# Turning the rows of layer 1 by DMA, with the attention sums nine steps behind

## The chip, the cores and the metric

The kernel runs on one core of a Trainium2 chip. The metric is the device time of one execution in microseconds. A core has five engines with their own instruction queues that meet only by semaphores: TensorE (PE, matmuls), VectorE (DVE), ScalarE (ACT), GpSimd (POOL) and SyncE (SP, which here only issues DMAs). DMAs issued by one engine go into that engine's queue and are carried out by 16 shared DMA engines; q1 is SP's queue, q10 ACT's, q0 GpSimd's.

## The reference

Two graph layers over N = 3327 nodes with D = 256 features and a dense 0/1 matrix adj of N x N:

```python
h = relu(layernorm(x))
s_left, s_right = (h @ W_sa) @ a_left, (h @ W_sa) @ a_right
e = where(adj != 0, exp(-leaky_relu(s_left[:, None] + s_right[None, :], 0.01)), 0)
x_a = e / (e.sum(1) + 1e-5) @ (h @ W_sa)
x_b = adj @ (h @ W_gcnb) + b_gcnb
x = x + sigmoid(gate_a * x_a + gate_b * x_b)      # gates: sigmoids of projections of adj @ h and h
h = relu(layernorm(x))
x = x + relu(((dinv * (adj + I) * dinv) @ h + h) @ W1 + b1)
```

## The kernel before, in words

The nodes are 26 tiles of 128, taken as 13 pairs (PAIRS = 13, LAST = 12). float32 values are kept as two float16 (or bfloat16) numbers, a rounded first half (HI) and the rest (LO), and multiplied by several matmuls.

**Front of layer 1.** For each pair s: DVE takes the statistics of the rows (row_stats), POOL the inverse deviation, DVE the shift (minus_mean), ACT normalizes into hf (norm). PE turns hf by four float32 transposes into the PSUM tile tp (turn), ACT rounds tp into hTh (turned), DVE takes the rest into hTl (turned_second); both lie in hTx. PE then multiplies by the weights: dense(s), 12 matmuls of 512 columns into the two PSUM banks of dn, and project(s), 8 small ones into pw, the scores. ACT copies each bank of dn into HI (first_halves), DVE takes the rest into LO (second_halves); dense(s+1) waits for the same bank's second half. DVE takes the scores out of pw (take_scores).

**The sums of pair m.** For every neighbour pair u: ACT makes the scores' exponentials Z (leaky, expo), DVE masks them by the adjacency (mask) and splits them (split into E), PE sums: neighbours(m, u), 8 matmuls with adj into accA, and unit(m, u), 12 matmuls with Z and E into accE. The adjacency of pair m is loaded by POOL's DMAs (load_adj), turned by DVE (turn_adj, two chunks, six and seven pairs), and stored for layer 2 by SP (keep_adj). Output row sets m = 1 to 12 follow m = 0; neighbours(m+1, u) run between the units of m, except that all of neighbours(1, u) stand ahead of unit(1, 0).

**The order.** Every engine's program is written out by hand. The front is a loop over steps s; in it, PE does dense(s), turn(s+2), and from s = 4 on the sums of pair m = 0 four steps behind: neighbours(0, s-4), unit(0, s-5). keep_busy(n) are n filler matmuls on a constant tile whose results nobody reads.

**Layer 2** (names ending in 1) uses the other way of turning rows: ACT rounds hf into hfx (rounded1), DVE puts the rest beside it (rounded_second1), and SP turns both by one transposing DMA from hfx into hTx (turn_rows1), so that PE does no transposes there. The DMAs of SP ahead of all this are the loads of x, then bgrep and b1rep (two vectors of 256, each repeated on 128 partitions), which nobody needs before about 100 us.

## Time and profile before

| | us |
|---|---|
| runs of the kernel before (3) | median 614.05, 613.71 to 614.7 |
| the profiled execution | 614.12, span 612.3 |
| TensorE busy | 593.1 (97%) |
| VectorE busy | 429.1 (70%) |
| ScalarE busy | 358.2 (59%) |
| GpSimd busy | 258.0 (42%) |

Busy shares are of the whole span; the profile's windows give them stretch by stretch. All times in the rows below are microseconds from the span's start unless marked ns. A timeline row of PE shows the time until the result of a matmul is written; matmuls overlap, so the step from one start to the next is what one costs.

### The profile page before, as it was taken

The page shows a single profiled execution, that of the slowest core. Times are in us where ns is not written, and L with a number is a line of the kernel's source. Part 1 is how long each engine was busy: PE and PEld are TensorE (multiplying, and loading weights), DVE is VectorE, ACT ScalarE, POOL GpSimd, SP SyncE. Part 2 cuts the span into 40 slices and gives each one's busy share as a digit, 9 for nine tenths or more (in the row PEclk, how much of TensorE's full clock was granted, in tenths as well). Part 3 has the DMA queues.
Part 4 walks back from the last instruction along what each step waited for, and adds up shares of the span by engine and source line. Part 5 has one row for each costly group of instructions (what it writes and reads, how often), then busy time and mean ns, then how long its engine had stood idle before and what let it go on. Part 6 is the DMA issues. An engine that isn't in the chain of part 4 may idle for free.

```text
span 612.3 us, 13252 instructions
## 1 busy us (share of the span) xinstructions
PE 593.1 (97%) x5265; PEld 508.2 (83%) x5265; DVE 429.1 (70%) x826; ACT 358.2 (59%) x865; POOL 258.0 (42%) x360
## 2 busy tenths in 40 slices
PE   6778999999999999999999999999999999999996
PEld 4446678888888888888888888888888888888886
DVE  5897877999999999899989989988753222111111
ACT  3576767798978888787978788979642000000000
POOL 3637333453544434343534376313132284435433
PEclk9999999999999999999999999999999999999999
DMA  8907396976574656556564745010300386545401
GB/s 198 220 5 112 54 223 184 203 106 172 79 181 74 168 93 151 113 130 120 123 148 95 163 79 78 2 19 2 128 2 18 102 326 214 167 165 192 146 19 34
DMA packets 55801, 73.60 MB, mean 120 GB/s; under 512 B 20027, under 2 KB 47933, under 8 KB 54331
## 3 DMA queue, kind: packets, MB, share of 16 engines
q0 software_dynamic: 28544, 22.15, 25.5%
q1 hardware_dynamic: 24754, 46.42, 23.5%
q10 hardware_dynamic: 2441, 4.20, 2.2%
q8 instruction: 41, 0.67, 0.5%
q14 instruction: 21, 0.17, 0.1%
HBM read 69.31 MB, written 22.16 MB: 149 GB/s over the span
## 4 chain that ended last, share of the span: by engine, by line
PE 91%; DVE 4%; issue 2%; DMA 2%; ACT 1%; ACTq 0%; DVEq 0%
PE accA L759 12%; PE accE L781 12%; PE accE L783 12%; PE accE L782 12%; PE accA L760 12%; PE accA L825 7%; PE accA L826 7%; PE accE L826 4%; PE accE L825 4%; PE accA L733 1%; PE accA L735 1%; PE accA L734 1%; DMA late<-in_L_gnn_W_gcnb_dram 1%; PE pw L798 1%; PE accA L841 1%
## 5 line engine op out<-in xcount | busy, mean ns | idle before, releaser
L781 PE MATMUL accE<-HI,Z 128*128 128x257 f16 x676 | 184.3, 273 | 0.0
L783 PE MATMUL accE<-HI,E 128*128 128x257 f16 x676 | 184.1, 272 | 0.0
L782 PE MATMUL accE<-LO,Z 128*128 128x256 f16 x676 | 183.9, 272 | 0.0
L548 ACT ACTIVATE Z<-LO,sr 128x256 f32<-128x256 f32 x338 | 151.4, 497 | 33.4 <-PE accE L783 33.4
L759 PE MATMUL accA<-HI,adjT 128*128 128x260 f16 x676 | 154.0, 273 | 0.0
L760 PE MATMUL accA<-LO,adjT 128*128 128x258 f16 x676 | 154.0, 273 | 0.0
L557 ACT ACTIVATE Z<-Z,sr 128x256 f32<-128x256 f32 x338 | 150.0, 496 | 0.2
L1036 DVE TENSOR_TENSOR Z<-adjT,Z 128x512 f32<-128x512 bf16 x169 | 127.8, 756 | 15.3 <-ACT Z L557 14.3
L1042 DVE TENSOR_TENSOR E<-Z 128x512 bf16<-128x512 f32 x169 | 129.0, 763 | 5.8
L370 POOL DMA_DIRECT2D stage<-in_adj_dram x96 | 59.6, 657 | 89.5 <-DVE adjT L1028 85.1
L826 PE MATMUL accA<-LO,adjT 128*128 128x256 f16 x416 | 91.6, 272 | 0.0
L825 PE MATMUL accA<-HI,adjT 128*128 128x256 f16 x416 | 91.6, 273 | 0.0
L759 PEld LDWEIGHTS accA<-HI,adjT 128*128 128x128 bf16 x676 | 65.8, 97 | 9.2
L760 PEld LDWEIGHTS accA<-LO,adjT 128*128 128x128 bf16 x676 | 65.8, 97 | 8.8
L782 PEld LDWEIGHTS accE<-LO,Z 128*128 128x128 bf16 x676 | 65.9, 98 | 8.4
L781 PEld LDWEIGHTS accE<-HI,Z 128*128 128x128 bf16 x676 | 65.8, 97 | 8.4
L783 PEld LDWEIGHTS accE<-HI,E 128*128 128x128 bf16 x676 | 65.7, 97 | 8.5
L1028 DVE STREAM_TRANSPOSE adjT<-stage 128x768 uint32<-128x768 uint32 (+1 forms) x52 | 50.9, 1016 | 0.0
L449 POOL TENSOR_SCALAR wx<-wx 128x512 f32<-128x512 f32 x13 | 12.7, 980 | 82.0 <-ACT wx L579 81.9
L825 PE MATMUL accE<-HI,stage 128*128 128x256 f16 x208 | 45.7, 272 | 0.0
L826 PE MATMUL accE<-LO,stage 128*128 128x256 f16 x208 | 45.7, 273 | 0.0
L480 POOL TENSOR_TENSOR late<-HI,LO 128x512 f32<-128x512 f16 x13 | 20.0, 1535 | 58.6 <-DVE wx L1214 28.4
(129 smaller groups left out, 746.3 us busy)
## 6 DMA issues: line engine op xcount, KB each, us to landing
adjT_store<-adjT SPq DMA_DIRECT2D x11, 1664.0 KB, 6.1
stage<-in_adj_dram POOLq DMA_DIRECT2D x48, 192.0 KB, 5.0
stage<-in_adj_dram POOLq DMA_DIRECT2D x36, 224.0 KB, 5.4
adjT<-adjT_store SPq DMA_DIRECT2D x7, 896.0 KB, 4.8
adjT<-adjT_store SPq DMA_DIRECT2D x7, 768.0 KB, 5.8
stage<-adjT_store SPq DMA_DIRECT2D x4, 896.0 KB, 6.6
stage<-adjT_store SPq DMA_DIRECT2D x4, 768.0 KB, 5.4
out_dram<-late ACTq DMA_DIRECT2D x11, 256.0 KB
```

The source lines that it names most:

```text
L370: pool.dma_start(stage[32 * b:32 * b + 32, :, :, w0:w1_], src).then_inc(adj_in[c], 16)
L548: ins = act.activation(Z[:, n % RING, v], slw[:, m], ACT.Relu, bias=sr99[:, t:t + 1], scale=1.0 - SLOPE)
L557: ins = act.activation(Z[:, n % RING, v], Z[:, n % RING, v], ACT.Exp, bias=sr01[:, t:t + 1], scale=-1.0)
L759: pe.matmul(dst[:, 0:D + 4], w, HI[:, t, ONE:HIW], start=(t == 0), stop=False)
L760: ins = pe.matmul(dst[:, 2:D + 4], w, LO[:, t, D:LOW], start=False, stop=(t == TILES - 1))
L781: pe.matmul(dst[:, 0:D + 1], zhi, HI[:, t, 0:D + 1], start=(t == 0), stop=False)
L782: pe.matmul(dst[:, 0:D], zhi, LO[:, t, 0:D], start=False, stop=False)
L783: ins = pe.matmul(dst[:, 0:D + 1], zlo, HI[:, t, 0:D + 1], start=False, stop=(t == TILES - 1))
L825: pe.matmul(dst, w, HI1[:, t, :], start=(t == 0), stop=False)
L826: ins = pe.matmul(dst, w, LO1[:, t, :], start=False, stop=(t == TILES - 1))
L1036: dve.tensor_tensor(Z[:, n % RING], rows, Z[:, n % RING], ALU.mult).then_inc(mask_ok, 1)
L1042: dve.tensor_tensor(E2[:, n % RING], Z[:, n % RING], hi, ALU.subtract).then_inc(e2_ok, 1)
```

## The change

Pairs 0 to 2 are still turned by PE. From pair 3 on (BY_PE = 3) layer 1 does what layer 2 does: ACT's rounded and DVE's rounded_second split hf into hfx (now two buffers), SP's turn_rows turns it into hTx, and PE's dense and project wait for the DMA's semaphore (turned_in). The turn of pair i waits until dense(i-2), the last reader of the same half of hTx, is done. The sums of pair m = 0, with leaky, expo, mask and split, run nine steps behind the dense steps (BEHIND = 9) and not four. Statistics are taken one pair a step instead of in batches. The bias of the gates moves from DVE's take_scores into ACT's gate_exp. GpSimd's loads of the adjacency of pairs 1 and 2 and DVE's turn_adj move to later steps. The first store of the left scores is issued by ACT at s = 8. The comments that name an engine are added here.

```diff
-    BATCHES = [(0, 1), (1, 2), (2, 3), (3, 4), (4, 5), (5, 7), (7, 9), (9, PAIRS)]
+    BY_PE = 3
+    BEHIND = 9
...
+    def turn_count(i):
+        return 16 * len([j for j in range(BY_PE, i + 1) if j % 2 == i % 2])
...
-        hfx = sb("hfx", [P, 2, HALVES, 2, P], F16)
+        hfx = sb("hfx", [P, 2, 2, HALVES, 2, P], F16)
...
+            def turn_rows(i):                                        # sync
+                sp.wait_ge(hfl_ok, i - BY_PE + 1)
+                sp.wait_ge(dn_ps, 2 * i - 2)
+                sp.dma_start_transpose(hTx[:, i % 2].rearrange("p a h (e i) -> p (a h e) i", e=2),
+                                       hfx[:, i % 2].rearrange("p a h e d -> p (a h e d)")).then_inc(hT_in[i % 2], 16)
...
             sp.dma_start(bgrep[:], ...)
             sp.dma_start(b1rep[:], ...)
-
-            sp.wait_ge(adj_in[1], adj_count(1, 1))
+            for i in range(BY_PE, PAIRS):
+                turn_rows(i)
             spread_left(0)
             keep_adj(0)
+            store_left(1)
             spread_left(1)
...
-            loads = {4: (1, 0), 5: (1, 1), 9: (2, 0), 10: (2, 1)}    # gpsimd
+            inv_std(3)
+            inv_std(4)
+            loads = {BEHIND: (1, 0), BEHIND + 1: (1, 1)}
             for s in range(PAIRS):
                 score_parts(s)
-                if s == 0:
-                    inv_stds(3)
-                if s in (0, 1, 2, 4):
-                    inv_stds({0: 4, 1: 5, 2: 6, 4: 7}[s])
                 gate_columns(s)
+                if s >= 1 and s + 4 < PAIRS:
+                    inv_std(s + 4)
                 if s in loads:
                     load_adj(*loads[s])
+            load_adj(2, 0)
+            load_adj(2, 1)
...
+            def rounded(i):                                          # scalar
+                act.wait_ge(hf_ok, 2 * i + 2)
+                if i - 2 >= BY_PE:
+                    act.wait_ge(hT_in[i % 2], turn_count(i - 2))
+                act.activation(hfx[:, i % 2, 0] ..., hf[:, i % 2] ..., ACT.Copy).then_inc(hfh_ok, 1)
...
             norm(0)
+            first_weights(0)
             turned(0)
-            first_weights(0)
             first_weights(1)
             norm(1)
-            for s in range(PAIRS + 5):
+            for s in range(PAIRS + BEHIND + 1):
                 if s == 0:
-                    first_halves(0)
-                if s + 1 < PAIRS:
+                    first_half(0, 0)
+                    first_half(0, 1)
+                if s + 1 < BY_PE:
                     turned(s + 1)
                 if s + 2 < PAIRS:
                     norm(s + 2)
-                if 0 <= s - 4 < PAIRS:
-                    expo(0, s - 4)
                 if 0 < s < PAIRS:
-                    first_halves(s)
-                if s == 1:
+                    first_half(s, 0)
+                if BY_PE <= s + 2 < PAIRS:
+                    rounded(s + 2)
+                if 0 < s < PAIRS:
+                    first_half(s, 1)
+                if s == 3:
                     left_first()
-                if 0 <= s - 3 < PAIRS:
-                    leaky(0, s - 3)
-                if s == 9:
+                if s == 8:
+                    act.wait_ge(srw_ok, SPREAD[0][1])
+                    act.dma_start(left_store(0), srw[...]).then_inc(sl_out[0], 16)
+                if 0 <= s - BEHIND < PAIRS:
+                    expo(0, s - BEHIND)
+                if 0 <= s - BEHIND + 1 < PAIRS:
+                    leaky(0, s - BEHIND + 1)
+                if s == PAIRS:
                     first_weights(2)
...
+            def turned_in(i):                                        # tensor
+                if i < BY_PE:
+                    pe.wait_ge(hTl_ok, i + 1)
+                else:
+                    pe.wait_ge(hT_in[i % 2], turn_count(i))
...
             keep_busy(8)
+            spread_weights(0, 2, 1)
             turn(0)
-            spread_weights(0, 2, 1)
             keep_busy(20)
             for s in range(PAIRS):
                 dense(s)
                 if s == 0:
                     turn(1)
                     project(0)
+                    turn(2)
                     spread_weights(2, 4, 2)
-                    keep_busy(4)
-                if s == 1:
+                if s == 2:
                     widen_first()
-                if s + 2 < PAIRS:
-                    turn(s + 2)
-                if 1 <= s < 4:
-                    keep_busy(4)
-                if s >= 4:
-                    neighbours(0, s - 4)
-                if s >= 5:
-                    unit(0, s - 5)
+                if 1 <= s < BEHIND:
+                    keep_busy(3)
+                if s >= BEHIND:
+                    neighbours(0, s - BEHIND)
+                if s > BEHIND:
+                    unit(0, s - BEHIND - 1)
                 if s + 1 < PAIRS:
                     project(s + 1)
-            for u in range(PAIRS - 4, PAIRS):
+            for u in range(PAIRS - BEHIND, PAIRS):
                 neighbours(0, u)
                 unit(0, u - 1)
...
             def take_scores(i):                                      # vector
                 dve.wait_ge(proj, i + 1)
-                dve.tensor_reduce(out=scored[:], ...).then_inc(scored_ok, 1)
-                dve.wait_ge(scored_ok, i + 1)
-                dve.tensor_tensor(srw[:, 2 * i:2 * i + 2, :], scored[:], bias6 ..., ALU.add).then_inc(srw_ok, 1)
+                dve.tensor_reduce(out=srw[:, 2 * i:2 * i + 2, :], ...).then_inc(srw_ok, 1)
...
-            turns = {3: (0, 0), 4: (0, 1), 8: (1, 0), 9: (1, 1)}
-            for s in range(1, PAIRS + 4):
+            turns = {BEHIND - 1: (0, 0), BEHIND: (0, 1), PAIRS: (1, 0), PAIRS + 1: (1, 1)}
+            for s in range(1, PAIRS + BEHIND):
                 if s < PAIRS:
                     take_scores(s)
-                if s + 1 < PAIRS:
+                if s + 1 < BY_PE:
                     turned_second(s + 1)
-                if s in (2, 3, 5):
-                    minus_mean({2: 4, 3: 6, 5: 7}[s])
                 if s < PAIRS:
-                    second_halves(s)
-                for j in (2 * s + 3, 2 * s + 4):
-                    if j < PAIRS:
-                        row_stats(j)
+                    second_half(s, 0)
+                    second_half(s, 1)
+                if BY_PE <= s + 2 < PAIRS:
+                    rounded_second(s + 2)
+                if s + 3 < PAIRS:
+                    minus_mean(s + 3)
+                if s == 1:
+                    diagonal_first()
+                    scales(2, 4, 2)
+                if s + 4 < PAIRS:
+                    row_stats(s + 4)
...
                 if s in turns:
                     turn_adj(*turns[s])
-                if 0 <= s - 4 < PAIRS:
-                    mask(0, s - 4)
-                    split(0, s - 4)
+                if 0 <= s - BEHIND < PAIRS:
+                    mask(0, s - BEHIND)
+                    split(0, s - BEHIND)
```

Three places show how rows move. SP's queue from the vectors on, before:

```order
L312 DMA bgrep<-in_L_gnn_b_gcnb_dram 128x256
L313 DMA b1rep<-in_L_gnn_b_dram 128x256
L301 DMA sl_store<-srw 128x12x1
L304 DMA LO<-sl_store 128x1536
L309 DMA adjT_store<-adjT 128x3328
```

and now:

```order
L331 DMA bgrep<-in_L_gnn_b_gcnb_dram 128x256
L332 DMA b1rep<-in_L_gnn_b_dram 128x256
L323 DMA_TRANSPOSE hTx<-hfx 128x8x128 x10
L317 DMA LO<-sl_store 128x1536
L328 DMA adjT_store<-adjT 128x3328
L311 DMA sl_store<-srw 128x12x1
```

Ten transposes have come in between b1rep and the stores.

TensorE between dense(2), whose last matmul is the first row, and the projection of pair 3, before:

```order
L735 MATMUL accA<-wh,hTx 128x512
L685 MATMUL tp<-ident,hf 128x128 x4
L697 MATMUL accA<-ones 128x256 x4
L713 MATMUL pw<-w6s,hTx 128x18
L715 MATMUL pw<-w6s,hTx 128x12
```

and now:

```order
L781 MATMUL accA<-wh,hTx 128x512
L767 MATMUL accE<-diag,ones 128x256
L737 MATMUL accA<-ones 128x256 x3
L759 MATMUL pw<-w6s,hTx 128x18
L761 MATMUL pw<-w6s,hTx 128x12
```

The four transposes are gone, the widening of the first left scores (accE) stands here, and three fillers instead of four; the projection now waits for the DMA.

VectorE in one step of the loop, s = 5, before (scores, tp's rest, shift, LO, mask, split):

```order
L995 TENSOR_REDUCE scored<-pw 128x12
L998 TENSOR_TENSOR srw<-scored,bias 128x12
L987 TENSOR_TENSOR hTx<-tp,hTx 128x512
L940 SCALAR_TENSOR_TENSOR nmr<-mv,rstd 128x8
L1011 TENSOR_TENSOR LO<-accA,HI 128x512 x2
L1036 TENSOR_TENSOR Z<-adjT,Z 128x512
L1042 TENSOR_TENSOR E<-Z 128x512
```

and now, in one of the steps 2 to 7:

```order
L1033 TENSOR_REDUCE srw<-pw 128x12
L1046 TENSOR_TENSOR LO<-accA,HI 128x512 x2
L1052 TENSOR_TENSOR hfx<-hf,hfx 128x2x2x128
L981 SCALAR_TENSOR_TENSOR nmr<-mv,rstd 128x2
L972 BN_STATS bst<-xs 128x6 x2
L976 BN_AGGR mv<-bst 128x2 x2
```

rounded_second (hfx) stands behind the two second halves (LO) of the step, and the statistics behind it; mask and split are left to later steps.

## Rows read from the trace of the kernel before

**Rows 1.** Windows: us; busy and instructions of each engine; clock, DMA share, GB/s.

```profile
0.00:50.00 50.00, 35.87 (x234) 21.68 (x235) 38.87 (x130) 26.05 (x52) 24.26 (x67) 1.00 0.61 130
50.00:600.00 550.00, 549.72 (x4967) 480.01 (x4965) 388.46 (x693) 332.17 (x814) 231.72 (x293) 1.00 0.52 121
```

**Rows 2.** Waits of TensorE, 0 to 150 us: total, times, longest.

```profile
PE tp L685 <- DVE hTx L987: 6.0, 3, 3.0
```

**Rows 3.** Timeline of TensorE: start, us, line, operation, [idle before].

```profile
48.62 0.63 PE L685 MATMUL tp<-ident,hf 128*128 128x128 f32 x4 [2.99 <-DVE hTx L987]
...
51.48 0.38 PE L733 MATMUL accA<-wh,hTx 128*128 128x512 f16 x1
...
53.86 0.38 PE L735 MATMUL accA<-wh,hTx 128*128 128x512 f16 x1
...
67.77 0.38 PE L733 MATMUL accA<-wh,hTx 128*128 128x512 f16 x1
...
88.90 0.27 PE L759 MATMUL accA<-HI,adjT 128*128 128x260 f16 x1
...
91.10 0.27 PE L759 MATMUL accA<-HI,adjT 128*128 128x260 f16 x1
...
99.03 0.27 PE L759 MATMUL accA<-HI,adjT 128*128 128x260 f16 x1
```

**Rows 4.** Groups by line, 20 to 100 us, VectorE, then ScalarE: busy us, mean ns.

```profile
L1028 DVE STREAM_TRANSPOSE adjT<-stage 128x768 uint32<-128x768 uint32 (+1 forms) x10 | 9.6, 1001 | 0.0
...
L1036 DVE TENSOR_TENSOR Z<-adjT,Z 128x512 f32<-128x512 bf16 x13 | 8.8, 677 | 0.8 <-ACT Z L557 0.6
...
L930 DVE BATCH_NORM_STATS2 bst<-xs 128x6 f32<-128x256 f32 x20 | 7.3, 409 | 0.0
...
L548 ACT ACTIVATE Z<-LO,sr 128x256 f32<-128x256 f32 x28 | 12.6, 499 | 0.0
```

**Rows 5.** Timeline around dense(6): ScalarE's and VectorE's second half.

```profile
54.27 0.60 ACT L530 ACTIVATE HI<-accA 128x512 f16<-128x512 f32 x1 [0.70 <-PE accA L735]
...
54.90 0.69 DVE L1011 TENSOR_TENSOR LO<-accA,HI 128x512 f16<-128x512 f32 x1 [0.60 <-ACT HI L530]
```

**Rows 6.** The tile hfx, layer 2: ns min/median/max, and the turn's landing.

```profile
L1100 DVE TENSOR_TENSOR hfx<-hf,hfx x13: 681/1098/1101, 139.9 to 474.2; 128x512 f16<-128x512 f32 x13
...
DMA to landing us min/median/max: 3.1/3.1/4.7
```

**Rows 7.** SyncE's issue of b1rep; its count, KB, us from issue to landing.

```profile
15.84 0.58 SPq L313 DMA_DIRECT2D b1rep<-in_L_gnn_b_dram  x1
...
b1rep<-in_L_gnn_b_dram SPq DMA_DIRECT2D x1, 128.0 KB, 17.4
```

**Rows 8.** Windows, columns as in rows 1.

```profile
32.00:33.00 1.00, 1.00 (x6) 0.49 (x5) 0.96 (x6) 0.00 (x0) 0.00 (x0) 1.00 0.08 15
```

**Rows 9.** DMA queues, 32 to 33 us, then 33 to 34: packets, MB, share.

```profile
q0 software_dynamic: 10, 0.01, 5.0%
q1 hardware_dynamic: 8, 0.01, 2.7%
...
q0 software_dynamic: 14, 0.01, 7.7%
```

**Rows 10.** Layer 2, 141 to 144.5 us: SyncE's issue, GB/s in 40 slices.

```profile
142.40 0.57 SPq L309 DMA_DIRECT2D adjT_store<-adjT  x1
...
GB/s 0 0 0 0 0 0 0 0 0 0 0 0 0 0 20 132 228 211 219 217 219 202 205 217 211 196 205 187 823 1311 629 0 0 0 0 0 2130 304 0 0
```

**Rows 11.** Windows at the end; TensorE's fillers at the start and later.

```profile
609.00:610.00 1.00, 0.00 (x0) 0.00 (x0) 0.00 (x0) 0.00 (x0) 0.00 (x0) 1.00 0.06 11
610.00:611.00 1.00, 0.00 (x0) 0.00 (x0) 0.00 (x0) 0.00 (x0) 0.00 (x0) 0.75 0.25 73
...
1.64 3.60 PE L697 MATMUL accA<-ones 128*128 128x256 bf16 x16 [1.64 <-POOL ident L355]
...
18.87 0.60 PE L697 MATMUL accA<-ones 128*128 128x256 bf16 x4
```

More of the change, by code:

```diff
@@ L281, in out_count, with left_store @@
             return 16 * sum({LAST: 3, LAST - 2: 2}.get(ORDER[j], 1) for j in range(k + 1) if j % 2 == b)
+        def left_store(g):
+            a, b = SPREAD[g]
+            return bass.AP(sl_store.tensor, 2 * P * a, [[1, P], [P, 2 * (b - a)]])
         block = ctx.enter_context(nc.Block())
@@ L562, in gate_exp @@
                 act.wait_ge(zg_ok, m + 1)
-                act.activation(eg[:], zg[:], ACT.Exp, scale=-1.0).then_inc(eg_ok, 1)
+                if m == 0:
+                    act.wait_ge(nbias_ok, 1)
+                for k in range(2):
+                    ins = act.activation(eg[:, :, k], zg[:, :, k], ACT.Exp, bias=nbias[:, k:k + 1], scale=-1.0)
+                ins.then_inc(eg_ok, 1)
             def gated_b(m):
@@ L1005, in diagonal_first, with second_half, rounded_second @@
                 ins.then_inc(diag_ok, 1)
-            def second_halves(i):
-                for e in range(2):
-                    dve.wait_ge(hi_ok, 2 * i + e + 1)
-                    first = bass.AP(HI[:].tensor, (2 * i + e) * HIW, [[TILES * HIW, P], [G0, 2], [1, D]])
-                    dve.tensor_tensor(LO[:, 2 * i + e, 0:2 * D].rearrange("p (k d) -> p k d", k=2),
-                                      bank(dn, e).rearrange("p (k d) -> p k d", k=2), first,
-                                      ALU.subtract).then_inc(lo_ok, 1)
+            def second_half(i, e):
+                dve.wait_ge(hi_ok, 2 * i + e + 1)
+                first = bass.AP(HI[:].tensor, (2 * i + e) * HIW, [[TILES * HIW, P], [G0, 2], [1, D]])
+                dve.tensor_tensor(LO[:, 2 * i + e, 0:2 * D].rearrange("p (k d) -> p k d", k=2),
+                                  bank(dn, e).rearrange("p (k d) -> p k d", k=2), first,
+                                  ALU.subtract).then_inc(lo_ok, 1)
+            def rounded_second(i):
+                dve.wait_ge(hfh_ok, i - BY_PE + 1)
+                dve.tensor_tensor(hfx[:, i % 2, 1].rearrange("p h e d -> p e h d"),
+                                  hf[:, i % 2].rearrange("p e (h d) -> p e h d", h=HALVES),
+                                  hfx[:, i % 2, 0].rearrange("p h e d -> p e h d"),
+                                  ALU.subtract).then_inc(hfl_ok, 1)
             def turn_adj(m, c):
```

123 lines of the change are left out of this document (59 added, 64 removed).

## The prediction

> **What bounds the kernel now.** I read the windows first. TensorE (PE) is busy 35.87 of the first 50 us and 549.72 of the next 550 [rows 1]. After 50 us every PE microsecond is a kernel microsecond; the only idle time to win is the 14.1 us before it. What PE does later, from the first matmul of neighbours(1,0) on, is the same in both kernels. So the whole question is when that matmul starts: 99.03 us now [rows 3].
>
> Then the waits and PE's timeline, to see what those 14.1 us are. The largest is the transposes into tp waiting for VectorE (DVE), 6.0 us [rows 2], the longest 2.99 us at 48.62 [rows 3]. From dense(6) at 51.48 on, PE has no gap: a step lasts 5.43 us (dense(9) is at 67.77, three steps later) [rows 3]. Useful work of a step: dense 12 matmuls of 0.216 us, 2.59 (the first starts at 51.48, the last at 53.86); neighbours and unit 2.20 together (88.90 to 91.10) [rows 3], of which 8 matmuls in 20 are neighbours, 0.88 and 1.32; the projection 0.2. The transposes are the remaining 0.44.
>
> **What it removes.** Ten of thirteen turns by PE: 10 x 0.44 = 4.4 us, and with them ten copies out of tp on ScalarE (ACT) and ten subtractions on DVE; rounded and rounded_second, of the same shape, come in their place. take_scores loses a small addition. The statistics one pair a step cost GpSimd some more small instructions beside others' work: nothing. The new order of the first weights and turn(0) may start dense(0) up to 1 us earlier; this, too, comes to nothing, because of the next wait.
>
> **What it adds: a wait for a DMA queue.** Pair 3's rows are now turned by a DMA on SP's queue. I take its inputs as ready at about 26.7: dense(2) starts at 25.55 now, about 24.7 with the earlier start, and rounded_second(3) stands behind second_half(1,1), which ends 1.3 us after that, plus its own 0.65; 2 us more or less change nothing as long as the queue is the later one. With an idle queue a turn takes 3.1 us from issue to landing (once 4.7) [rows 6]; but SP's queue isn't idle. Behind the loads of x stand bgrep and b1rep, and b1rep, issued at 15.84, lands 17.4 us later, at 33.2 [rows 7]. The share of the 16 DMA engines is only 0.08 at 32 to 33 us, about one engine [rows 8], and in that microsecond SP's queue (q1) still has 8 packets and GpSimd's (q0) 10 [rows 9]: one engine is late with both queues. Does a transpose overtake what stands ahead of it in its queue? In layer 2 SP issues a transpose and, at 142.40, a 1.66 MB store; the rate stays near 210 GB/s for 13 slices of 87 ns, 1.2 us, and only then jumps to 823 and 1311 [rows 10]: the store waited for the transpose. A transpose behind b1rep should wait the same way on the late engine. It would start there at 33.2, needs 1.2 to 1.3 us of its own, and shares that engine with the rest of q0 (14 packets at 33 to 34 [rows 9]), 1.1 us: 35.6, and 0.3 for the semaphore and the projection. **dense(3) at 35.9** (bounds: 30.1 = 26.7 + 3.1 + 0.3 if nothing holds it, 37 if the queue behind GpSimd's loads is slower).
>
> On this order the Trainium skill (DMA: Bandwidth & Descriptors, Queues, rings and completion order) says that on each DMA engine the descriptors of one issuing queue are consumed in ring order; by the page the turn lands at 35.6, and the trace's store behind a transpose agrees.
>
> **The steps from dense(3) to dense(9).** There is now a loop through four engines: dense(s) must be done before ACT and DVE take its halves; only behind them does DVE do rounded_second(s+2), only then can SP issue turn s+2, and dense(s+2) waits for it. From rows: ACT takes the second half of dense(6) at 54.27, 2.79 us after that dense began, DVE at 54.90, 3.42 after, done at 4.03 [rows 3, 5]. Then 0.65 for DVE's split into hfx (681 ns the shortest, 1.10 the median [rows 6]; the median stands beside GpSimd's long operations of layer 2, which this stretch lacks), 3.1 for the turn [rows 6], 0.3 for semaphore and projection: 8.15 us for two steps with the hand-overs. dense(4) follows dense(3) by 3.1 (2.59 + three fillers 0.33 + projection 0.2), dense(5) stands at +8.2, dense(7) at +16.3, dense(9) at +24.45. The even chain is the same length (ACT's norm of 1.0 us waits for minus_mean, which stands behind rounded_second, but stays inside it). DVE's own load of a step is 0.2 + 1.3 + 0.65 + 0.1 + row_stats 0.95 = 3.2 [rows 4], below 4.08, so the turn sets the pace: 35.9 + 24.45 = 60.35. That is 7.4 us sooner than now (67.77), but neighbours(0,0..4) and unit(0,0..3) are still owed, 9.7 us of PE work that is now already done there.
>
> **The clock.** From about 28.2 (dense(2), the widening matmul, three fillers) to 35.6 PE has nothing: over 7 us. At the end of the kernel, with PE idle, the granted clock is 1.00 until 610 and averages 0.75 from 610 to 611 [rows 11]: it drops to the low level (1.2 GHz) when PE is left idle, while the present 2.99 us gap costs nothing (the matmuls after it keep their 0.216 us). At the start, 16 filler matmuls take 3.60 us, 0.22 each, where 4 later ones take 0.60 with their tail, near 0.11 [rows 11]: at the low level everything is twice as long. dense(3) would take up to 5.2. I charge **1.8 us** (nothing if the clock holds, 2.6 if all of dense(3) is slow); it lies on the loop above, so it moves all that follows. dense(9): 62.15.
>
> The Trainium skill (TensorE: Matmul & The Clock Gate, Why this matters for your kernels) warns against long idle gaps between bursts of matmuls, since the clock then falls back to half. By it the 1.8 is due; without it the sum would be 1.8 smaller.
>
> **From dense(9) to neighbours(1,0).** PE still has 4 dense, 3 projections, 13 neighbours and 13 units: 10.4 + 0.6 + 11.4 + 17.2 = 39.6 us. Where it waits: DVE does turn_adj(0,0) (two rows of 1.0, or 0.9 for the six-pair form [rows 4]) behind row_stats(12), and take_scores(9) and the second halves of 9 behind that: dense(10) follows by 4.55 for 3.7 of work. turn_adj(0,1), 2.0, plus mask and split, 1.37 [rows 4], come before unit(0,0): dense(11) 5.9 later for 5.0 of work; then 5.0, 4.8. In the nine pairs left, turn_adj(1,0), turn_adj(1,1) and second_weights(2) push mask and split behind PE, 1.7 more. Sum 4.55 + 5.9 + 5.0 + 4.8 + 19.8 + 1.3 + 1.7 = 43.05. ACT's 2.0 us a pair and DVE's 1.4 are below PE's 2.20.
>
> neighbours(1,0) starts at 62.15 + 43.05 = 105.2 against 99.03: **+6.2 us**. Made against the profiled execution's own 614.12 (span 612.30) this is 620.3; the runs' median of 614.05 is 0.07 lower, so 620.2. Put as a balance: 4.4 of transposes are gone, but the wait for pair 3 and the loop leave PE waiting longer than it did.
>
> sl_store now leaves on ACT's queue behind first_half(8,1), and SP's spread_left(0) and keep_adj(0) behind the tenth turn, about 70 us; both end over 20 us ahead of leaky(1,0), so nothing waits. turn_adj(2,0) needs that keep_adj, also long done.
>
> **Rivals.**
> (a) The turn isn't held: it overtakes b1rep, or none of its packets lies on the late engine. For it: by 32 us all engines but one have finished [rows 8]. Against: the store behind the transpose [rows 10]. dense(3) at 30.1 to 31.7, no long gap, the clock holds: 30.1 + 24.45 + 43.05 = 97.6, -1.4 us: 612.6. This is the case on the other side, **faster**; it decides where dense(3) starts before 31.5 with the clock up (99.03 - 67.5). Chance 0.14; its upper end, 31.7, is no change.
> (b) Held in part, dense(3) at 32 to 34, the clock stays up: 614.6 to 616.6. Chance 0.12.
> (c) Held, clock stays up: 618.4. Chance 0.12.
> (d) The loop is slower than 8.15: DVE's split at 1.10 (+0.45 in each of three rounds, 1.35), a turn beside GpSimd's adjacency loads at 4.7 instead of 3.1 (+1.6), the whole dense(3) slow (+0.8): up to 624. Chance 0.14.
> (e) Forecast, held with the clock down: 618.8 to 622. Chance 0.48.
>
> **Numbers.** The measurement tells 0.2%, 1.2 us, from nothing. Faster is the low end of (a), 0.08, and 0.05 for a loop much shorter than I think; same is the rest of (a) and the low end of (b), 0.13; slower 0.74. The range takes in most of (b) and (d): 614.8 to 623.4.
>
> **What would show it.** SP's first transpose issued at 26 to 28 us but landing some 8 us later; PE idle from about 28 to 35.6 for a DMA; granted clock below 1.00 around 32 to 38; dense(3), (5), (7), (9) about 8.2 apart, each behind a DMA wait; PE solid from about 65; neighbours(1,0) near 105. The forecast is wrong if the first turn lands by 31, or if the steps go at DVE's 3.2 us: the loop would then be 5 us shorter and the change near no change.

## The result: 636.4 us, 22 us more than before

The changed kernel takes 636.42 us (median of 4 runs, 634.76 to 637.17), the kernel before, run beside it, 613.88 (median of 4): a ratio of 1.0352, with a 95% interval from 1.0328 to 1.0376. Forecast were 620.2 us, 614.8 to 623.4: the sign was right, the size was missed by 16 us. The profiled execution of the changed kernel took 636.03 us, its span is 634.2 (before: 612.3).

The windows first. The columns are those of [rows 1].

```profile
0.00:50.00 50.00, 36.44 (x212) 19.69 (x213) 31.79 (x106) 22.92 (x43) 21.97 (x70) 0.83 0.76 151
50.00:100.00 50.00, 38.97 (x282) 23.82 (x280) 35.02 (x69) 32.23 (x71) 21.52 (x59) 0.90 0.70 117
100.00:150.00 50.00, 44.09 (x379) 37.82 (x378) 35.50 (x63) 31.88 (x83) 17.76 (x23) 0.93 0.80 168
150.00:600.00 450.00, 449.86 (x4099) 399.21 (x4097) 322.69 (x572) 275.36 (x685) 186.78 (x210) 1.00 0.49 119
```

TensorE was solid from 50 us on [rows 1]; now it is so only from 150 on. Between 50 and 150 it is idle for 16.9 us and its clock is below 1.00. The waits of TensorE up to 150 us (total, times, longest) name two of them, and neither was there before [rows 2]:

```profile
PE pw L759 <- DMA hTx<-hfx: 16.9, 7, 6.3
PE accE L827 <- DVE wm L1122: 5.9, 1, 5.9
```

And TensorE's timeline gives the places: the projection before dense(3), dense(4), dense(9), the projection before dense(10) and dense(10) itself, neighbours(1,0), and unit(1,0).

```profile
33.47 0.19 PE L759 MATMUL pw<-w6s,hTx 128*128 128x18 bf16 x1 [6.18 <-DMA hTx<-hfx]
...
39.67 0.38 PE L779 MATMUL accA<-wh,hTx 128*128 128x512 f16 x1
...
60.59 0.38 PE L779 MATMUL accA<-wh,hTx 128*128 128x512 f16 x1
...
71.43 0.20 PE L759 MATMUL pw<-w6s,hTx 128*128 128x18 bf16 x1 [6.31 <-DMA hTx<-hfx]
71.67 0.59 PE L779 MATMUL accA<-wh,hTx 128*128 128x512 f16 x1
...
112.45 0.27 PE L805 MATMUL accA<-HI,adjT 128*128 128x260 f16 x1
...
130.01 0.37 PE L827 MATMUL accE<-HI,Z 128*128 128x257 f16 x1 [5.91 <-DVE wm L1122]
```

dense(9) starts at 60.59, near the forecast (62.15). Then it goes wrong. The transpose of pair 10 holds TensorE for 6.31 us, the clock falls (a matmul of dense(10) is 0.59 us long instead of 0.38), and neighbours(1,0) starts at 112.45 where 105.2 was forecast and 99.03 measured before [rows 3]. A second wait of 5.91 us, in no part of the forecast, comes before unit(1,0). The balance of the two spans: +13.4 up to neighbours(1,0), +5.9 for that wait, and +2.5 for the clock behind it (0.50 from 130 to 135 us); sum 21.8, measured 21.9.

**The first stall.** The issue of the first small store, on ScalarE's queue, and, from the DMA issues, the landing (the last number, us) of that store and of the transpose that SyncE issues at 61.30:

```profile
59.28 0.40 ACTq L655 DMA_DIRECT2D sl_store<-srw  x1
```

```profile
sl_store<-srw ACTq DMA_DIRECT2D x1, 6.0 KB, 11.6
...
hTx<-hfx SPq DMA_TRANSPOSE x1, 10.1
```

The store ends at 70.9, the transpose at 71.4. In layer 2 before, a transpose took 3.1 [rows 6]. When did its data move? The GB/s from 62 to 66 us, in 40 slices of 0.1 us, then the windows behind:

```profile
GB/s 0 0 0 0 20 151 220 218 218 218 205 197 187 113 36 13 0 0 0 0 3 10 110 69 110 187 118 0 3 18 188 3 10 0 0 0 0 0 0 0
```

```profile
66.00:69.00 3.00, 0.00 (x0) 0.00 (x0) 2.97 (x4) 1.09 (x2) 2.40 (x4) 0.64 0.00 0
69.00:72.00 3.00, 0.57 (x9) 0.34 (x10) 0.41 (x2) 0.00 (x0) 0.00 (x0) 0.50 0.65 49
```

The 0.26 MB of the transpose (all that moved in these 4 us) are through by 65.3. Then nothing moves on any of the 16 engines for more than 3 us, with a store, two transposes and loads outstanding, and only when the small store lands does the transpose count as landed. By the packet records its data had moved; the semaphore came with the store. The store's own packets had moved even earlier, between 60.2 and 61.3 us, before the transpose was issued. Its queue in that window:

```profile
q10 hardware_dynamic: 1552, 0.01, 64.4%
```

These are its 1536 pieces of 4 bytes and 16 more. It counts as landed 9.6 us later. So the others wait for its completion, not for the moving of its bytes.

The Trainium skill has the rule, which the forecast left out (DMA: Bandwidth & Descriptors, Queues, rings and completion order): the increment of a semaphore is a strongly ordered write, it lands only after every earlier write of that DMA engine, "across its queues". The trace agrees: a store on ScalarE's queue held a transpose on SyncE's. The rule by itself doesn't say why the loads issued from 65.88 us on had not begun to move by 69.

**The second stall**, before unit(1,0), is a chain through all engines. VectorE's, GpSimd's and ScalarE's timelines, in the order of time:

```profile
112.87 1.84 DVE L1070 STREAM_TRANSPOSE adjT<-stage 128x768 uint32<-128x768 uint32 x2 [6.36 <-DMA stage<-in_adj_dram]
...
115.00 2.39 POOL L389 DMA_DIRECT2D stage<-in_adj_dram  x4 [17.07 <-DVE adjT L1070]
117.47 0.22 POOL L482 TENSOR_SCALAR nbias<-bias 128x2 f32<-128x2 f32 x1
...
117.78 0.48 ACT L594 ACTIVATE eg<-zg,nbias 128x2 f32<-128x2 f32 x2 [12.78 <-POOL nbias L482]
```

VectorE waits for pair 2's adjacency. The four loads of the first chunk, issued from 92.2 on, take 10.7 to 18.8 us, those of the second, from 95.5 on, 17.8 to 20.0; the second small store is under way from 85.09 to 100.4. Here it isn't only the completion that is late. The windows (the last number is GB/s) show that next to nothing moves before the store has landed:

```profile
91.00:100.00 9.00, 7.39 (x66) 6.07 (x65) 8.86 (x14) 8.87 (x22) 4.87 (x8) 1.00 0.29 6
100.00:113.00 13.00, 13.00 (x120) 11.49 (x119) 6.47 (x11) 4.90 (x13) 0.00 (x0) 1.00 1.09 279
```

Behind it the loads share the engines with the 2.4 MB of spread_left(1) and keep_adj(1), which SyncE issues at 100.39 and 100.75. GpSimd issues load_adj(3,0) behind that, and the negation of the gate's biases, which the change put behind this load, comes at 117.47. The gate of pair 0 on ScalarE (idle for 12.78 us by then) gets its last input there, 2.5 us after its arguments, and everything of pair 1 stands behind the gate.

### The profile page after: what moved, and what is told of

The parts are those of the page before. It is cut to its first block, busy times and chain, and to the rows that moved or that the text cites. A ratio compares the mean times of both kernels' runs of the same rounds, so it can differ in the third digit from the quotient of the medians.

```text
span 634.2 us, 13210 instructions
## 1 busy us (share of the span) xinstructions
PE 598.8 (94%) x5233; PEld 506.7 (80%) x5233; DVE 430.0 (68%) x816; ACT 362.4 (57%) x878; POOL 258.8 (41%) x371
## 4 chain that ended last, share of the span: by engine, by line
PE 79%; DMA 6%; ACT 2%; DVE 2%; issue 1%; POOL 1%; ACTq 0%; DVEq 0%
PE accE L827 11%; PE accE L829 11%; PE accE L828 11%; PE accA L805 10%; PE accA L806 10%; PE accA L872 7%; PE accA L871 7%; PE accE L872 4%; PE accE L871 4%; DMA stage<-in_adj_dram 3%; DMA hTx<-hfx 3%; PE pw L844 1%; PE accA L887 1%; PE pw L845 1%; PE pw L846 1%
## 5 line engine op out<-in xcount | busy, mean ns | idle before, releaser
L1084 DVE TENSOR_TENSOR E<-Z 128x512 bf16<-128x512 f32 x169 | 131.4, 777 | 5.8
L806 PEld LDWEIGHTS accA<-LO,adjT 128*128 128x128 bf16 x676 | 65.8, 97 | 9.1 <-issue 0.3
L872 PEld LDWEIGHTS accA<-LO,adjT 128*128 128x128 bf16 x416 | 40.7, 98 | 4.7
```

Source lines behind the costliest of these rows:

```text
L806: ins = pe.matmul(dst[:, 2:D + 4], w, LO[:, t, D:LOW], start=False, stop=(t == TILES - 1))
L872: ins = pe.matmul(dst, w, LO1[:, t, :], start=False, stop=(t == TILES - 1))
L1084: dve.tensor_tensor(E2[:, n % RING], Z[:, n % RING], hi, ALU.subtract).then_inc(e2_ok, 1)
```

## The experiments

All runs have their own runs of the kernel before beside them; the ratio is to those. "Expected" is what was on record ahead of each.

| run | us, median | ratio, 95% interval |
|---|---|---|
| first small store behind the transposes | 631.7 | 1.0277, 1.0253 to 1.0300 |
| first small store in 128 pieces | 630.85 | 1.0261, 1.0233 to 1.0289 |
| biases negated ahead of pair 2's loads | 631.59 | 1.0280, 1.0245 to 1.0315 |
| 60 fillers in step 2 | 632.02 | 1.0266, 1.0196 to 1.0335 |
| bgrep and b1rep behind the transposes | 636.54 | 1.0366, 1.0339 to 1.0394 |
| chunk (0,1) loaded in step 4 | 635.92 | 1.0369, 1.0340 to 1.0397 |
| first store and pair 1's loads late | 648.44 | 1.0555, 1.0530 to 1.0579 |
| four mends together | 624.61 | 1.0189, 1.0132 to 1.0246 |
| DMA transposes, whole-row stores | 627.02 | 1.0206, 1.0175 to 1.0237 |
| same, biases early, 40 fillers | 621.8 | 1.0113, 1.0059 to 1.0166 |
| DMA transposes, four steps behind | 638.37 | 1.0398, 1.0370 to 1.0426 |
| TensorE transposes, nine steps behind | 621.69 | 1.0124, 1.0096 to 1.0153 |
| same, whole-row stores | 611.36 | 0.9955, 0.9939 to 0.9970 |
| before, whole-row stores | 614.43 | 1.0012, 0.9997 to 1.0027 |
| TensorE transposes, four steps behind | 619.1 | 1.0079, 1.0055 to 1.0104 |
| same, SyncE's wait put back | 613.64 | 0.9983, 0.9967 to 1.0000 |
| same, biases negated at the start | 611.75 | 0.9943, 0.9921 to 0.9966 |

### Is it the small store that holds transpose 10?

Two runs: the store moved away in time, and the same bytes in fewer pieces.

```diff
-                if s == 8:
-                    act.wait_ge(srw_ok, SPREAD[0][1])
-                    act.dma_start(left_store(0), srw[...], ...).then_inc(sl_out[0], 16)
...
             for i in range(BY_PE, PAIRS):
                 turn_rows(i)
+            store_left(0)
             spread_left(0)
```

> The first store of the left scores (1536 elements of 4 bytes) moves from ScalarE's queue at step 8 to SyncE's, behind all ten turns. Theory (the small store holds the turn of pair 10, issued 2 us behind it, and all other DMAs for some 8 us): that turn lands 3 to 4 us after issue and not 10.1, TensorE's idle gap of 6.3 us before project(10) and the half clock after it are gone; 6.3 + 2.6 us less, about 627.5. Rival (GpSimd's adjacency loads, issued 4.6 us behind that turn, delay it): the landing stays near 10 us and the time near 636.

The second run stores 48 bytes next to each other from each partition of another tile, so pairs 1 to 6 get other left scores.

```diff
-                    act.dma_start(left_store(0), srw[...], allow_slow_non_contiguous=True)
+                    act.dma_start(bass.AP(sl_store.tensor, 2 * P * SPREAD[0][0], [[12, P], [1, 12]]),
+                                  rstd[:, SPREAD[0][0]:SPREAD[0][1]].rearrange("p u e -> p (u e)"))
```

> The store stays on ScalarE's queue at step 8 with the same 6 KB, but takes 48 contiguous bytes a partition from the tile rstd (so pairs 1 to 6 get other numbers for their left scores): 128 pieces and not 1536. Theory (the number of 4-byte pieces holds the DMA engines): turn of pair 10 lands in 3 to 4 us, time near 627.5. Rival (any DMA on a second queue just ahead of a turn holds it): lands near 10 us, time near 636.

Both gain some 5 us: 631.7 and 630.85. With the wide store, the store lands in 1.8 us, and the two transposes issued beside it in 3.1:

```profile
hTx<-hfx SPq DMA_TRANSPOSE x2, 3.1
sl_store<-rstd ACTq DMA_DIRECT2D x1, 6.0 KB, 1.8
```

So it is the 1536 pieces of 4 bytes, not the store or its place. But only 5 of the expected 8.9 us came out. One part is that a later transpose waits instead; another is the scatter of dense(3) told below, which puts dense(9) of the profiled run with the store moved at 62.12, 1.5 later. In the run with the store moved, TensorE's next wait for a DMA is that of pair 12, and the landings of the transpose and of GpSimd's loads issued beside it, from 72 to 76 us, show what it stands beside:

```profile
81.30 0.18 PE L756 MATMUL pw<-w6s,hTx 128*128 128x18 bf16 x1 [3.08 <-DMA hTx<-hfx]
```

```profile
stage<-in_adj_dram POOLq DMA_DIRECT2D x3, 224.0 KB, 8.3
stage<-in_adj_dram POOLq DMA_DIRECT2D x1, 223.5 KB, 10.8
hTx<-hfx SPq DMA_TRANSPOSE x1, 8.5
```

The moved store, issued at 74.05, stands beside that transpose too. With the wide store no 4-byte store is near, and pair 12's transpose still takes 8.3 us.

### Do GpSimd's loads hold transposes 11 and 12?

The store as above, and load_adj(1,0) and load_adj(1,1) from steps 9 and 10 to behind the loop.

```diff
-            loads = {BEHIND: (1, 0), BEHIND + 1: (1, 1)}
+            loads = {}
...
+            load_adj(1, 0)
+            load_adj(1, 1)
             load_adj(2, 0)
```

> The first store behind the transposes, as in the run with the later store, and besides GpSimd's loads of pair 1 behind the loop, ahead of those of pair 2. If these loads are what holds the transpose of pair 12 (8.5 us there), it lands in 3.1 to 4 and dense(12) starts 3 us earlier, at about 78; what follows pays for it, as adjacency tiles of pairs 1 and 2 arrive some 8 us later: 630 to 640. If the transpose is held by something else, it still takes 8 us or more.

They do: with the loads away, the transposes from 62 us on land in 3.1 us and the last, pair 12's, in 4.6, and dense(12) starts at 77.79, 3.7 earlier than in the run above. What follows pays far more for it, as TensorE waits for pair 1's adjacency: 648.44, above the 630 to 640 expected.

```profile
102.61 0.39 PE L826 MATMUL accE<-HI,Z 128*128 128x257 f16 x1 [16.76 <-DVE E L1083]
```

### What holds the transpose of pair 3?

My forecast blamed b1rep. It and bgrep were moved:

```diff
-            sp.dma_start(bgrep[:], ...)
-            sp.dma_start(b1rep[:], ...)
             for i in range(BY_PE, PAIRS):
                 turn_rows(i)
+            sp.dma_start(bgrep[:], ...)
+            sp.dma_start(b1rep[:], ...)
```

> Only the loads of bgrep and b1rep move, behind the ten transposes on SyncE's queue. If b1rep's transfer is what holds the transpose of pair 3, it is issued at about 23 to 25 and lands about 3.1 after, so that dense(3) starts at 29 to 31 where it was 33.7, and the run is 2 to 3 us shorter (634). If the transpose waits for GpSimd's adjacency loads of pair 0 instead, it lands at 33.4 as before, and the time is 636.

Refuted. With neither in the queue the transpose, issued at 25.86, lands 7.5 us later, and the time stays at 636.54. TensorE resumes where it did:

```profile
33.39 0.20 PE L759 MATMUL pw<-w6s,hTx 128*128 128x18 bf16 x1 [5.50 <-DMA hTx<-hfx]
```

Then the other load that moves there, GpSimd's chunk (0,1), was asked for in step 4 instead of at 17.4 us.

```diff
-            load_adj(0, 1)
...
-            loads = {BEHIND: (1, 0), BEHIND + 1: (1, 1)}
+            loads = {4: (0, 1), BEHIND: (1, 0), BEHIND + 1: (1, 1)}
```

> The changed kernel with GpSimd's load of the second adjacency chunk of pair 0 (896 KB) asked for in step 4 of the loop in place of 17.4 us. If the transpose of pair 3 stood behind the volume of x and adjacency that moves until 32, it lands some 4 us earlier (0.9 MB at 220 GB/s), dense(3) starts at 29 to 30 where it was 33.7, and a transpose of pair 5 to 7 lands in 5 to 8 us where it was 3.1; the time is 632 to 637. If the transpose does not depend on that volume, dense(3) starts at 33 to 34 as before and the time is 636 to 640.

Transpose 3, issued at 26.61, now lands in 4.3 us and dense(3) starts at 31.15 (33.70 before this edit). The same load, now at 41.95, holds pair 7's transpose instead: the first row is that of pair 3, the second that of pair 7.

```profile
hTx<-hfx SPq DMA_TRANSPOSE x1, 4.3
...
hTx<-hfx SPq DMA_TRANSPOSE x1, 7.8
```

The time, 635.92, is unchanged: a load that takes 8 us holds a transpose wherever it stands. dense(3) itself scatters over the runs that leave this place alone, from 33.1 to 36.3.

### The clock in dense(3), and the gate's biases

```diff
                 if 1 <= s < BEHIND:
-                    keep_busy(3)
+                    keep_busy(60 if s == 2 else 3)
```

> 60 filler matmuls and not 3 behind dense(2), some 6.4 us at full clock, so that TensorE isn't idle while it waits for the turn of pair 3. Theory (the clock fell in that wait and dense(3) ran at half rate): dense(4) follows dense(3) by 3.1 us and not 6.0, everything behind is up to 2.9 us earlier: 633.5 to 634.5. Rival (dense(3) is off the path, the turns set the pace whatever the clock): 636.

The granted clock is 1.00 from 30 to 40 us where it was 0.50 and 0.54, and dense(3) to dense(4) take 3.12 us where it was 5.97 (first matmul of each):

```profile
34.66 0.38 PE L779 MATMUL accA<-wh,hTx 128*128 128x512 f16 x1
...
37.78 0.38 PE L779 MATMUL accA<-wh,hTx 128*128 128x512 f16 x1
```

So idling cost 2.9 us by the clock. dense(9) then starts at 58.94, 24.28 us after dense(3): that is the loop without the clock (24.45 in the forecast). The runs of this kernel scatter, 625.71 to 634.33, so of the 4.4 us gained in the median only the 2.9 are shown.

The next run moves one instruction ahead of load_adj(2,0) on GpSimd.

```diff
+            pool.wait_ge(bias_in, 32)
+            pool.tensor_scalar(nbias[:], bias2[:], -1.0, None, ALU.mult).then_inc(nbias_ok, 1)
             load_adj(2, 0)
             load_adj(2, 1)
...
             load_adj(3, 0)
-            pool.wait_ge(bias_in, 32)
-            pool.tensor_scalar(nbias[:], bias2[:], -1.0, None, ALU.mult).then_inc(nbias_ok, 1)
```

> GpSimd's nbias, which gate_exp(0) waits for, moves from behind load_adj(3, 0) to ahead of load_adj(2, 0). Theory (the second stall comes through turn_adj(2, 0), load_adj(3, 0) and nbias to gate_exp(0)): gate_exp(0) runs 0.3 us behind the gate's arguments and not 3.1, TensorE's stall before unit(1, 3) or so is 5.9 - 2.8 = 3.1 us, with the clock perhaps kept: 631 to 633.6. Rival (the late loads of pair 2 alone set that stall, GpSimd is beside the path): 636.

```profile
127.26 0.27 PE L827 MATMUL accE<-HI,Z 128*128 128x257 f16 x1 [2.81 <-DVE wm L1122]
```

The wait is 2.81 instead of 5.91, and as TensorE idles less its matmul has full length (0.27, not 0.37): 631.59, 4.8 less for one instruction of 0.22 us. The 2.81 that stay are put down to the late loads themselves; the run with whole-row stores below bears this out.

### Which part of the change costs what?

The next runs undo whole parts: transposes by TensorE again (BY_PE = PAIRS), or four steps behind again (BEHIND = 4, GpSimd's loads at their former steps, the first small store behind the transposes).

```diff
-    BY_PE = 3
+    BY_PE = PAIRS
...
+                if s >= 1 and s + 2 < PAIRS:
+                    turn(s + 2)
```

> The nine steps behind without transposes by DMA: all pairs are turned by TensorE again, as before the change, and the rest of the change stays. TensorE gets back some 1.1 us of work a pair for ten pairs. If the loss is in the transposes that transfers hold, TensorE waits for none in the loop, neighbours(1, 0) starts at 95 to 104 and the time is 612 to 620 (with the stall before unit(1, 0) still there, near 620). If the order with nine steps behind is itself dear, because the loads of pair 2 and the gate of pair 0 come later, the time stays above 625.

621.69. dense(9) starts at 50.67, ten us earlier than with DMA transposes, and TensorE's longest wait in the loop is 1.4 us. But then comes this, in SyncE's, VectorE's and TensorE's timelines: the end of the second small store (SyncE's next instruction waits for it), the turning of chunk (1,1), and TensorE.

```profile
86.05 0.32 SPq L317 DMA_DIRECT2D LO<-sl_store  x1
...
85.89 2.10 DVE L1072 STREAM_TRANSPOSE adjT<-stage 128x896 uint32<-128x896 uint32 x2 [9.15 <-DMA stage<-in_adj_dram]
...
89.35 0.40 PE L827 MATMUL accE<-HI,Z 128*128 128x257 f16 x1 [10.17 <-DVE E L1086]
```

Chunk (1,1) was issued at 60.7 to 62.5 and counts as landed up to 23.4 us later, within 0.2 us of the small store that was issued at 68.68, after it. The cure has to be a store with few pieces that computes the same: TensorE turns the 12 columns of scores, ScalarE copies them, and 12 rows of 512 bytes are stored.

```diff
+            def turn_left(g):
+                a, b = SPREAD[g]
+                pe.wait_ge(srw_ok, 13 if g else 9)
...
+                pe.transpose(pw[0:12, P:2 * P], srw[:, 2 * a:2 * b, 3], ident[:]).then_inc(slt_ps, 1)
...
+                    act.activation(slT[:], pw[0:12, P:2 * P], ACT.Copy).then_inc(slt_ok, 1)
+                    act.wait_ge(slt_ok, g + 1)
+                    act.dma_start(bass.AP(sl_store.tensor, 2 * P * SPREAD[g][0], [[P, 12], [1, P]]),
+                                  slT[:]).then_inc(sl_out[g], 16)
```

> Nine steps behind, all pairs turned by TensorE (621.7), and both stores of left scores in 12 pieces of 512 bytes. In the run without this the adjacency chunk (1, 1), asked for at 60.7, landed at 85.9, at the moment when the second small store landed (86.05), and TensorE waited 10.2 us for it. If the small store held it, that wait goes and the time is 609 to 613, below the kernel before. If the volume ahead of it in the queues is what made it late, the wait stays at 5 us or more and the time is 617 to 622.

611.36, ratio 0.9955: faster than the kernel before. Chunk (1,1), issued at the same place, lands in 8.4 and 9.7 us, the wait is gone, and neighbours(1,0) starts at 96.68:

```profile
stage<-in_adj_dram POOLq DMA_DIRECT2D x3, 224.0 KB, 8.4
stage<-in_adj_dram POOLq DMA_DIRECT2D x1, 223.5 KB, 9.7
```

```profile
96.68 0.27 PE L821 MATMUL accA<-HI,adjT 128*128 128x260 f16 x1
```

The same stores in the changed kernel, with its DMA transposes:

> The changed kernel, with both stores of left scores made of 12 pieces of 512 bytes where they were 1536 and 1536 pieces of 4: TensorE turns the 12 columns of scores, ScalarE copies them out of PSUM and stores them from its queue. All is computed as before. If the small pieces are the cause of both stalls, transpose 10 lands in 3 to 4 us, and the loads of pair 2 (12 to 20 us) land in 10 to 12, so that the stall before unit(1, 0) goes too: 636.4 less 8 less 4 to 6, or 622 to 625. If only the first stall hangs on them (as the run with the first store widened, 630.9, would have it), the time is 630 to 632 and the loads of pair 2 still take 15 us or more.

627.02: 9.4 less, so both small stores cost that much together (622 to 625 was expected). The slowest of pair 2's loads land in 11.9 us (first chunk) and 13.3 (second), where they took 18.8 and 20.0. The stall before unit(1,0) is gone, although the negation of the biases still stands behind load_adj(3,0): with the loads this much earlier it makes TensorE wait no more here. Most of the gain in the profiled run lies there, for neighbours(1,0) starts at 111.34, 1.1 before that of the changed kernel: dense(3) happened to start 2.6 later in it. The 15.7 us that separate this run from 611.36 are the transposes by DMA alone, all else being equal but the PSUM tile that the scores are turned in and the step (9 and 13, against 8 and 12) in which they are copied and stored. Their places: dense(3) starts at 36.32 against 29.55, the six steps to dense(9) take 26.91 us against 21.66, and neighbours(1,0) starts at 111.34 against 96.68.

And DMA transposes with four steps behind:

```diff
-    BEHIND = 9
+    BEHIND = 4
...
-            loads = {BEHIND: (1, 0), BEHIND + 1: (1, 1)}
+            loads = {4: (1, 0), 5: (1, 1), 9: (2, 0), 10: (2, 1)}
```

> The other half of the change alone: transposes by DMA for pairs 3 to 12, but pair 0's sums and E four steps behind as before the change, with GpSimd's loads at their former steps, and the first small store behind the transposes. If transposes beside other transfers are the loss, dense(3) starts at 33 as well, two to four later transposes (of the pairs whose steps hold the loads of pairs 1 and 2) take 8 us or more, and the time is 630 to 645, above that of the whole change with the later store (631.7). If the nine steps are the larger part, it is 615 to 622.

638.37: more than the whole change. The transpose issued at 57.00, beside GpSimd's loads, takes 9.1 us; the last, issued between 83 and 85.3, takes 9.8 beside loads and the small store issued at 85.27. The order nine steps behind isn't what costs.

The kernel before, with turn_left and the stores of 12 rows as above:

> The kernel before with nothing changed but the stores of left scores, in 12 pieces of 512 bytes from ScalarE's queue. In its trace no engine on the path waits for a transfer between 50 and 100, so by that the time is that of before, 613.5 to 614.5. If the small stores delayed something there too, it falls to 611 or 612, and the gain of the nine steps behind with whole-row stores is the stores' alone.

614.43, no difference: in the kernel before the small stores cost nothing. So the 0.45% gained above isn't theirs.

### The line that kept the peace

Both parts are undone here, BY_PE = PAIRS and BEHIND = 4.

> The small edits of the change alone: TensorE turns all pairs, pair 0's sums and E are four steps behind, the small stores stand on SyncE's queue; what stays changed is the statistics of one pair a step, the gate's exponential in two with the negated biases behind GpSimd's load of pair 3, and fewer fillers. If these cost nothing the time is 613 to 615. If the negation behind the load costs what it cost in the changed kernel (2.8 to 5), it is 617 to 619.

619.1, so 5 us are in the small edits. Chunk (1,1), issued from 45.75 on, now takes up to 23.0 us, although TensorE does all transposes:

```profile
stage<-in_adj_dram POOLq DMA_DIRECT2D x1, 224.0 KB, 14.2
...
stage<-in_adj_dram POOLq DMA_DIRECT2D x1, 223.5 KB, 23.0
```

The small store stands at 45.34 in SyncE's queue, where it was at 60.47 before. The reason is a deleted line, ahead of spread_left(0): SyncE used to wait for pair 1's adjacency before it issued the store. It was put back.

```diff
+            sp.wait_ge(adj_in[1], adj_count(1, 1))
             store_left(0)
             spread_left(0)
```

> TensorE's transposes and four steps behind, as in the run of 619.1, with SyncE's removed wait for chunk (1, 1) back ahead of the first small store, and nothing else. If the small store beside the loads of pair 1 was the loss, chunk (1, 1) lands in 6 to 8 us again, the wait of 4.7 us at 75 us goes, and the time is 614 to 616; what is left over before is then the negated biases. If the wait does not matter, it is 619.

613.64. The chunk, now issued from 47.49 on, lands in 4.5 and 6.6 us, and 5.5 us are back with one wait:

```profile
stage<-in_adj_dram POOLq DMA_DIRECT2D x3, 224.0 KB, 4.5
stage<-in_adj_dram POOLq DMA_DIRECT2D x1, 223.5 KB, 6.6
```

The wait also keeps spread_left(0) and keep_adj(0), 2.4 MB, behind these loads; without it they were issued at 56.53 and 56.91 and moved beside them. Between 46 and 58 us, with the small store under way, the mean was 9 GB/s; from 58 to 62 it was 196 and from 62 to 71 it was 329. So the small store accounts for the first 12 us of the late chunk, and what the 2.4 MB add behind it wasn't tried apart.

In the next, the two lines of the negation moved ahead of inv_std(0) besides:

> The same, and the negation of the gate's biases at the start of GpSimd's program, ahead of all loads of adjacency. If the small edits cost nothing else, this is the kernel before in all but name: 613 to 615. If it stays at 616 or more, the statistics of one pair a step or the gate's exponential in two cost something too.

611.75, ratio 0.9943: faster than before too. The negated biases cost 1.9 us here (the two intervals just don't overlap), and the other small edits cost nothing; they may gain.

### What mending gives

The first: the first store behind the transposes, bgrep and b1rep late, the biases early, 25 fillers. The second: whole-row stores, the biases early, 40 fillers.

> All repairs at once: the first store of left scores behind the ten transposes, the loads of bgrep and b1rep behind them too, the negation of the gate biases ahead of GpSimd's loads of pair 2, and 25 fillers in step 2. If each of the waits found so far is its own loss and they add, the time is 636.4 less about 8 (transpose 10 and its slow clock), 3 to 5 (the stall before unit(1, 0)), 3 (clock in dense(3)) and 2 (transpose 3 earlier): 618 to 620, neighbours(1, 0) from about 106. If they overlap, because what is released then waits for the transpose of pair 12 beside GpSimd's loads and for the loads of pair 2, it stays above 624, with PE waiting again at 75 to 80 us and before unit(1, 0).

> The changed kernel with whole-row stores, the negated biases ahead of the loads of pair 2, and 40 fillers in step 2 against the fall of the clock. What stays is that transposes stand behind other transfers: transpose 3 behind x and adjacency until 33 to 35, transposes 11 and 12 beside the loads of pair 1. By the sum of those waits (some 6 and 3 to 7 us) the time is 618 to 623, still above before. If the waits overlap with others that come out now, it stays at 625 to 628; if it comes under 614, the transposes by DMA cost nothing by themselves.

624.61 (619.52 to 628.77) and 621.8 (617.42 to 623.16). In the profiled execution of the second, TensorE's largest wait for a transpose is 2.0 us and neighbours(1,0) starts at 105.61, about where my sum had it (105.2). Even so it is 1.1% above the kernel before. With transposes by DMA no version came under it.

## Why the prediction was right in sign and wrong in size

**The queue is late for pair 3: right; its holder: wrong.** The step said that the transpose stands behind b1rep. It landed 8.0 us after its issue as forecast, and TensorE had nothing for 6.18 us, but with b1rep gone nothing changed. What holds it is GpSimd's chunk (0,1), on another queue: with that load moved it lands in 4.3. That the size came out is luck: b1rep (issued at 15.62, landed 16.6 later, at 32.2) and the last part of the chunk (13.3 after its issue at 19.1, at 32.4) end at almost the same time. dense(3) at 33.70 instead of 35.9, 2.2 early. I had taken order within one queue from the store behind a transpose [rows 10], and read the few packets left on q0 [rows 9] as a share of an engine (1.1 us) instead of as what completion waits for.

**The loop of 8.15 us: right.** 24.28 us from dense(3) to dense(9) with the clock up, 24.45 forecast.

**The clock: right mechanism, size low.** 1.8 charged, 2.6 on the way to dense(9) (26.89 less 24.28), which is what the prediction gave for a wholly slow dense(3). Together dense(9) came at 60.59, 1.6 before the forecast of 62.15; the two misses have opposite signs, so this, too, looks better than it was.

**From dense(9) to neighbours(1,0), 43.05: this is the step that failed**, with 51.86 measured. The 8.8 us too many are 6.31 of waiting for transpose 10 and the half clock behind it (0.50 from 69 to 76 us). The sum charged nothing for any transpose in this stretch. Two sentences are at fault, the second of them in rival (d). "sl_store now leaves on ACT's queue ... so nothing waits" asked who waits for the store, and not who completes behind it; it holds transpose 10 for 7 us more and drops the clock. And "a turn beside GpSimd's adjacency loads at 4.7 instead of 3.1 (+1.6)" took its bound from layer 2 [rows 6]; beside GpSimd's loads, with no 4-byte store near, transposes took up to 8.3 us (wide store) and 9.1 (four steps behind). In the changed kernel that of pair 12 took 5.4 and made TensorE wait for no more than 1 us; the price shows in the runs in which transpose 10 is prompt. The landing of 17.4 for b1rep itself [rows 7], a 128 KB load, was the nearer row, and it was read as a matter of that load.

**The stall before unit(1,0): not in the sum.** The new negation of the biases behind load_adj(3,0), and that the gate waits for it, wasn't costed at all; it cost 2.8 to 3.1 us of waiting and some clock. The loads of pair 2, later and slower, cost the other 2.8; with whole-row stores neither was left. The wait of 5.9 and 2.5 of half clock behind it are the other half of the miss: 8.8 - 1.6 + 5.9 + 2.5 = 15.6, against 15.7 in the profiled run.

**Ten transposes off TensorE, 4.4 us: the saving was real and worth nothing.** With transposes on TensorE and the order nine steps behind, a step takes 3.6 us (21.66 for six); with DMA it takes 4.05, since the loop goes through the queue's 3.1 us. With the DMA in the loop TensorE was no longer the bound of the stretch where the work was taken away.

**Rivals.** (d), up to 624, named two of the right mechanisms: the wholly slow dense(3) had the right size, the transposes beside loads were far too small; its slower split didn't come. (a), (b) and (c) fell, though dense(3) started within (b)'s range: the clock didn't stay up. What stays open: why dense(3) starts anywhere from 33.1 to 36.3 in runs that are alike there; why nothing at all moves between 66 and 69 us, and why the small store completes some 9 us behind its last packet, which the records of the queues don't tell; and what makes the versions at 611.4 and 611.75 faster than before (for the first, the order nine steps behind and the statistics of one pair a step weren't tried apart).

## What to carry to other kernels

When a transfer is put on the path, price it by the worst thing that is under way on any queue when it completes, not by its own median in a quiet stretch. When an edit moves or removes a wait on a DMA queue, ask what that wait kept apart. Of a store, count the pieces: 6 KB in 4-byte pieces take over three times as long as a transpose of 256 KB, and a transpose of 12 columns on TensorE, which makes 12 pieces of 512 bytes of them, takes the store off the path.

## What the hardware did that I had not expected

A store of 1536 pieces of 4 bytes lands in 10.5 us alone (in the run with the wait put back), in 11.6 beside a transpose and in 11.2 to 25.4 beside loads; the same 6 KB in 128 pieces lands in 1.8. Moving the pieces is the small part: when it is alone its 1552 packets are through by 58 us, the store lands at 66.4, and between 58 and 66 the rate is 0 GB/s. While it is under way, a transpose on another queue is not counted as landed though its packets have moved (10.1 us instead of 3.1), and loads hardly move at all: 6 GB/s from 91 to 100 us in the changed kernel, 9 from 46 to 58 in the run of 619.1, where they take up to 23.0 us instead of 6.6 (the last part of it beside 2.4 MB of other transfers). A transpose of 128x1024 16-bit numbers, 3.1 us alone, takes 5.4 to 9.1 beside 0.9 MB of loads on GpSimd's queue.
